# Two layers on one core: first loads in memory of their own, GpSimd's powers a step earlier, the scale inside the masked maximum

## What is computed

```
# part one: normalise x, shift, three projections r, k, v, scans along time -> rwkv
normed = (rwkv - mean) * rsqrt(var + 1e-5) * gamma + beta     # mean, var over all time steps of a head
x = x + normed @ W_o.T
# part two, on layernorm(x), twice
q, k, v = split(shift(h) @ wqkv)
q, k = l2norm(q) * qs, l2norm(k) * ks ; q, k = rotary_xpos(q, k)
sim = 8 * q @ k.T ; masked outside the window ; attn = softmax(sim) ; o = attn @ v
x = x + o @ wo
h = layernorm(shift(x)) * lg + lb ; x = x + (a * gelu(g)) @ w2 + b2,  a, g = split(h @ w1 + b1)
```

## Time and profile before

| | us |
|---|---|
| time, median of 3 runs (2927.34 to 2930.24) | 2929.16 |
| time of the profiled execution | 2932.18 |
| its span, first to last instruction | 2929.9 |
| PE busy (share of the span) | 2801.9 (96%) |
| ACT busy | 2325.5 (79%) |
| DVE busy | 2202.0 (75%) |
| POOL busy | 1571.2 (54%) |
| mean granted TensorE clock | 0.984 |

### The profile page before, as it was taken

The page is one execution under the profiler, slowest core; times in us unless marked ns, Lnnn a source line. Parts: engine busy times, 40 slices in busy tenths (PEclk is TensorE's granted clock), DMA queues, the critical chain, the costliest instruction groups (busy, mean ns, idle before and its releaser), DMA issues.

```text
span 2929.9 us, 67398 instructions
## 1 busy us (share of the span) xinstructions
PE 2801.9 (96%) x23076; PEld 2536.0 (87%) x23076; DVE 2202.0 (75%) x6587; ACT 2325.5 (79%) x5429; POOL 1571.2 (54%) x1524
## 2 busy tenths in 40 slices
PE   7999938899999999999999999999999999999998
PEld 6878826788998998899999899999999999999988
DVE  3979966887777778777777677777777777777773
ACT  4989946788888888888888788888888888888884
POOL 2313215656656665665566555555655655566553
PEclk9999968999999999999999999999999999999999
DMA  3252111111111111111111213111111111111111
GB/s 98 63 181 77 39 58 42 56 55 45 55 51 48 52 55 55 50 50 52 53 47 52 80 57 100 48 49 48 48 48 46 49 47 43 49 45 46 49 44 36
DMA packets 211302, 166.22 MB, mean 57 GB/s; under 512 B 21522, under 2 KB 206612, under 8 KB 209940
## 3 DMA queue, kind: packets, MB, share of 16 engines
q1 hardware_dynamic: 139284, 127.82, 14.3%
q10 hardware_dynamic: 71680, 34.10, 4.0%
HBM read 110.89 MB, written 42.58 MB: 52 GB/s over the span
## 4 chain that ended last, share of the span: by engine, by line
PE 64%; DVE 17%; POOL 6%; issue 6%; ACT 4%; DMA 1%; SPq 1%; DVEq 0%; ACTq 0%; POOLq 0%
PE ps L387 33%; PE ps L361 10%; PE ps L471 6%; PE ps L457 6%; DVE Sm L1072 5%; PE ps L445 5%; POOL rs L1218 3%; PE ps L430 2%; DVE Ar L1045 2%; POOL uTl L1304 1%; POOL r L1218 1%; DVE Gl L1145 1%; DVE Br L1046 1%; DVE Br L1047 1%; DVE oTl L1096 1%
## 5 line engine op out<-in xcount | busy, mean ns | idle before, releaser
L730 ACT ACTIVATE Sm<-Sm,nb,sc 128x256 f32<-128x256 f32 (+1 forms) x1024 | 597.4, 586 | 1.3 <-DVE nb L1079 0.5
L1072 DVE CUSTOM_DVE_ANT_0 Sm<-ps,mask 128x256 f32<-128x256 f32 (+1 forms) x1024 | 368.1, 414 | 79.6 <-PE ps L445 77.6
L387 PE MATMUL ps<-zTh,W1h 128*128 128x256 f32 (+1 forms) x1408 | 405.6, 288 | 0.0
L1145 DVE SCALAR_TENSOR_TENSOR Gl<-ps,vecs,Gl 128x256 f32<-128x256 f32 (+1 forms) x384 | 172.0, 475 | 304.2 <-PE ps L387 162.8
L387 PE MATMUL ps<-zTl,W1h 128*128 128x256 f32 (+1 forms) x1408 | 397.9, 283 | 0.0
L387 PE MATMUL ps<-zTh,W1l 128*128 128x256 f32 (+1 forms) x1408 | 393.4, 279 | 0.0
L1218 POOL TENSOR_TENSOR rs<-rs,mhalf 128x16 f32<-128x16 f32 x128 | 372.3, 2909 | 0.0
L710 ACT ACTIVATE sq<-ps 128x512 f32<-128x512 f32 x256 | 151.7, 593 | 261.7 <-PE ps L387 258.2
L1304 POOL TENSOR_TENSOR uTl<-Gl,uTh 128x512 fp32r<-128x512 f32 (+1 forms) x192 | 211.2, 1106 | 251.4 <-ACT uTh L798 199.1
L387 PE MATMUL ps<-WQh,hTh 128*128 128x512 f32 x768 | 341.5, 445 | 3.1 <-DVE hTl L1029 3.1
L387 PE MATMUL ps<-WQl,hTh 128*128 128x512 f32 x768 | 305.8, 398 | 0.0
(11 more groups left out here) (187 smaller groups left out, 8796.3 us busy)
## 6 DMA issues: line engine op xcount, KB each, us to landing
oF<-ro_scratch ACTq DMA_DIRECT2D x256, 128.0 KB, 3.0
tb<-tab SPq DMA_DIRECT2D x128, 128.0 KB, 2.3
xc<-x SPq DMA_DIRECT2D x32, 256.0 KB, 3.0
rwkv_scratch<-rw SPq DMA_DIRECT2D x32, 256.0 KB, 2.5
rk<-rwkv_scratch SPq DMA_DIRECT2D x64, 128.0 KB, 2.3
xin<-x SPq DMA_DIRECT2D x64, 128.0 KB, 2.2
x_scratch<-x SPq DMA_DIRECT2D x64, 128.0 KB, 1.7
y_scratch<-os SPq DMA_DIRECT2D x64, 128.0 KB, 4.0
```

What stands on the lines that cost most here:

```text
L387: ins = pe.matmul(dst, L(a), R(b), start=start and i == 0, stop=stop and i == 2)
L730: act.activation(Sm[:, h, c0:c1_], Sm[:, h, c0:c1_], ACT.Exp, bias=nb[:, h:h + 1], scale=sc[:, n % 4, h:h + 1], accum_out=sm[:, n % 2, h:h ...
L1072: dve.tensor_tensor_reduce(Sm[:, h, c0:c1_], PS[:, bank["scores", n, q, h % 2], (h // 2 % 2) * 256 + c0:(h // 2 % 2) * 256 + c1_], mask[:, ...
L1145: dve.scalar_tensor_tensor(out=Gl[0:v, j % 4, :], in0=s, scalar=V("b1a", 6 * l + j, 0, v), in1=gl, op0=ALU.add, op1=ALU.mult).then_inc(S[" ...
```

## The change

There are three groups of edits.

The tiles `mask`, `qsks`, `xin`, `rk`, `nF`, `nT`, `tb` and `rt` are allocated ahead of part one's tiles, so they share memory with nothing. SP issues the loads of mask, `qsks`, the first `rk` and the first `xin` in part one's last step, ahead of the last `store_rw`, and no longer waits for `end`. ACT waits for `g2` at 10 in place of `end` at 3. PE, DVE and POOL still wait for `end`.

On POOL `scale` moves from step n+3 to step n+2, right behind `rot`. Its power is cut in two, 8 values for k first, then the product of k, then 8 values for q; `sc` gets the factor -8. The steps behind it in the same turn of the loop are `table`, `zT_lo` (every other step) and `root0`.

On DVE the fused instruction takes `sc` as a scale per row, `Sm` = (scores + mask) x `sc`, with the minimum in place of the maximum, and leaves the result in `nb` itself; L1079 and `mx` are gone. ACT's `exp` has the constant scale -1. `pre_y` moves from the start of DVE's step to the place right behind the maxima.

```diff
+        mask = sb("mask", [2, 256])
+        qsks = sb("qsks", [2, 256])
...
         with ExitStack() as c1:
...
-            w.wait_ge(S["end"], 3)
+            w.wait_ge(S["g2"], 10)
...
-                w.wait_ge(S["nb"], 2 * n + q + 1)
+                w.wait_ge(S["mx"], 8 * n + 4 * q + 4)
...
-                                   scale=sc[:, n % 4, h:h + 1], accum_out=sm[:, n % 2, h:h + 1]).then_inc(S["ex"], 1)
+                                   scale=-1.0, accum_out=sm[:, n % 2, h:h + 1]).then_inc(S["ex"], 1)
...
-                        mask[:, n % 2, c0:c1_], 1.0, -3.0e38, ALU.add, ALU.max, mx[:, h:h + 1]).then_inc(S["mx"], 1)
...
-                dve.scalar_tensor_tensor(out=nb[:, r], in0=mx[:, r], scalar=-1.0, in1=sc[:, n % 4, r], op0=ALU.mult,
-                                         op1=ALU.mult).then_inc(S["nb"], 1)
+                        mask[:, n % 2, c0:c1_], sc[:, n % 4, h:h + 1], 3.0e38, ALU.add, ALU.min,
+                        nb[:, h:h + 1]).then_inc(S["mx"], 1)
...
-                if live(1) and t - 1 < NG:
-                    pre_y(t - 1)
...
                     masked_max(t - 4, 0)
                     masked_max(t - 4, 1)
+                if live(1) and t - 1 < NG:
+                    pre_y(t - 1)
...
-                inv_sqrt(rs[:, n % 2, :]).then_inc(S["rs"], 1)
+                inv_sqrt(rs[:, n % 2, 8:16]).then_inc(S["rs"], 1)
...
+                inv_sqrt(rs[:, n % 2, 0:8]).then_inc(S["rs"], 1)
+                w.wait_ge(S["rs"], 2 * n + 2)
...
-                if live(3):
-                    scale(t - 3)
...
                     rot(t - 2)
+                    scale(t - 2)
...
+                if t - 4 == NCH - 1:
+                    sp.dma_start(mask[:, :, :], mask_d).then_inc(S["ld2"], 16)
+                    sp.dma_start(qsks[:, :, :], qsk).then_inc(S["ld2"], 16)
+                    load_rk(0)
+                    load_x(0)
                 if 0 <= t - 4 < NCH:
                     store_rw(t - 4)
-
-            w.wait_ge(S["end"], 3)
```

More of the change, by code:

```diff
@@ L198, in build @@
         gsh = sb("gsh", [NB, 2])
+        mask = sb("mask", [2, 256])
+        qsks = sb("qsks", [2, 256])
+        xin = sb("xin", [2, 256])
+        rk = sb("rk", [2, 2, 128])
+        nF = sb("nF", [2, 128])
+        nT = pair("nT", [2, 128])
+        tb = sb("tb", [2, 256])
+        rt = sb("rt", [2, 256])
         def V(name, i, lo=0, hi=128):
@@ L1068, in masked_max @@
                 w.wait_ge(S["ld2"], 32)
+                w.wait_ge(S["sc"], n + 1)
+                w.wait_ge(S["ex"], 8 * (n - 1) + 4 * q + 4)
                 for h in (4 * q, 4 * q + 2, 4 * q + 1, 4 * q + 3):
```

44 lines of the change are left out of this document (14 added, 30 removed).

## The result

| | before | after |
|---|---|---|
| median of the runs (4 each) | 2929.7 us | 2907.56 us (2905.66 to 2908.88) |
| ratio after / before, 95% interval | | 0.9924 [0.9909, 0.9940] |
| span of the profiled execution | 2929.9 us | 2905.6 us |
| mean granted clock | 0.984 | 0.986 |

The change makes the kernel 22.1 us faster by the medians, 24.3 us by the spans. The forecast was 28.4 us of gain, 2900.8 us, with a range of 2888 to 2918, and faster.

What follows compares the result with a forecast made beforehand. PE's own work bounds the second layer; gains lie in the seam, filling and first layer. 5.9 + 15 + 7 + 0.5 (the end) = 28.4 us off 2929.16 gives 2900.8 us, range 2888 to 2918.

Steps and rivals of the forecast that it cites:

- The seam: Between the parts: with `rk` loaded early, `nTl` starts at 413.40 in place of 419.27, a gain of 5.9 us.
- The powers: POOL: a power of 8 values costs 1656 ns; PE's 11.8 us of waits for the product of k should go.
- The filling: 420 to 600 us, while the pipeline fills: PE's waits for the product of k and `x2` shrink, gaining 15 us.
- The lower bound of 6 us: Filling: gain if DVE's step, near 14 of 16 us, bounds at once; the rival that DVE or POOL does had 0.14.
- The first layer: PE's waits for DVE's rotary product, 10.9 us in all, shrink by 7 us.
- I take 0: DVE's fused maximum: the scale per row adds between 0 and 57 ns each, taken as 0.
- 4.9 us for each 10 ns: Price of a slower fused instruction, eight times per step on DVE, over about 61 steps of filling and first layer.
- the signs that were named for being wrong: Fused instruction above 430 ns or further apart, `y` far above 0.41 us, or a new first-layer PE wait over 1 us each.
- The port race: First layer: `y` 0.3 us later loses the port to POOL's `uTl` in 26 MLP steps, +15 us, 2923; chance 0.09.
- The slower instruction as the case on the other side: DVE's fused instruction with a scale per row is slower, deciding from 70 ns, 2956 at twice 57 ns; chance 0.06.
- ACT's `exp`: Loses a value per row, from 590 to about 500 ns; counted as cover, no time gained.
- The second layer: PE is never idle there (busy 799.90 of 800 us), so nothing is gained.

Runs made afterwards that it cites:

- y_idle_onepow: The changed kernel with `y` from step 12 on ahead of DVE's `glu` and one power of 16 values in place of two of 8; 2895.19 us, ratio 0.9883.
- mixed_onepow: The changed kernel with `y` ahead of `glu` from step 12, one power of 16, scale in the maximum for windows 0 to 7 only; 2891.66 us, ratio 0.9871.
- onepow: The changed kernel with one power of 16 values in place of two of 8, at the new place; 2903.28 us, ratio 0.9906.
- y_idle: The changed kernel with `y` from step 12 on ahead of DVE's `glu` instead of behind the maxima; 2898.33 us, ratio 0.9889.
- imm_scale: The changed kernel with the fused instruction multiplying by the constant -1 in place of the row's value `sc`; 2896.26 us, ratio 0.9883.
- no_seam: The changed kernel without the early loads: SP and ACT wait for `end`, first loads behind all stores; 2911.78 us, ratio 0.9937.
- y_old: The changed kernel with `y` back at the start of DVE's step, the powers at their new place; 3120.1 us, ratio 1.0649.
- scale_old: The changed kernel with `scale`, still cut in two, back in the later step behind `root1`; 2913.16 us, ratio 0.9939.
- seam_only: The kernel before with only the early loads, their own memory and ACT's wait for `g2`; 2923.26 us, ratio 0.9976.
- unfused: The changed kernel with the plain maximum, the small `nb` instruction and `exp`'s scale per row back; 2903.82 us, ratio 0.9911.
- y_idle_unfused: The changed kernel with `y` from step 12 on ahead of `glu` and the maximum without the scale, small `nb` back; 2896.07 us, ratio 0.9881.
- best: The changed kernel with `y` from step 12 on ahead of `glu`, the maximum without the scale and one power of 16; 2895.7 us, ratio 0.9884.

## Why the prediction was nearly right

**The seam: right.** Forecast 5.9 us and `nTl` at 413.4; measured 413.53 and a lead of 5.86, by itself worth a ratio of 0.9976. The early issues cost nothing, and the last store's end never showed.

**The powers: right in size.** A power of 8 values was put at 1656 ns and took 1647. The wait for the product of k went. `z` was to lose up to 0.5 us a step, half counted, which is 1.25 us in five steps. Only the first of the two `z` instructions of a window meets the product; it takes 0.83 us and not 0.35, so it loses 0.48, and in the filling that cost 1.5 us, in windows 7 to 9. The forecast was close here.

**The filling: right, 15 us forecast, 16.3 measured, and by its terms too, with some luck.** Forecast were 6 us where PE waits for the first two products of k; measured are 6.3 up to window 2. Forecast were 8 in the later steps, which have 6.9 from window 5 to 10; 2.3 come between and 0.7 behind. For the clock 1 us was counted: the 180 us of the filling have 0.91 and 0.92 of granted clock, 32.4 and 28.8 us at the lower level, so 1.8 us at most. The luck is in the sum: two kernels with the same instructions there (`y_idle_onepow` and `mixed_onepow`) differ by 2.5 us by their clock, so a match to 1.3 us is closer than one execution can promise. No run parts the new place of `y` from the cut of the power. The lower bound of 6 us gave DVE near 14 of a step's 16 us; the row named for it, 131.80 of 180 us, is 11.7 of 16.

**The first layer: the step that failed.** The term was 7 us; 2.4 came. The step was "I take 0" for the value per row of the fused instruction, with 57 ns as the far end. It is 62 ns, so the far end was the truth. The nearest row, L1145, which has such a value and a PSUM input, had said 475 ns; the reason for setting it aside, that it is another operation, was weak. The price of it was also wrong, the other way: 4.9 us for each 10 ns, on all 61 steps, would have made 29 us. Measured is 11 us by the time and 10.0 by the growth, since PE's wait in the first layer is only 0.28 us a time, and a DVE that is earlier by more than that gains nothing. The term had a second fault. It took PE's mean wait of 0.44 us as the thing to be shortened, but that mean is of 21 waits near 0.3 and four of 1.0 to 1.5; the four went, and the 21 needed DVE to be 0.3 us earlier, which it wasn't. Two of the signs that were named for being wrong did come: the fused instruction above 430 ns, and `y` far above 0.41 us. PE's wait for the rotary product came to 6.9 us, where about 3 was to show the forecast right.

**The port race: a rival that happened, at a lower price.** It was put at 0.3 us of delay for `y` and +15 us. `y` did come late, lost 0.41 us, and PE still waited 25 times; but `u_tail` (0.42 us) and `oT_lo` (0.69 us) ran free behind it. So PE's wait became 0.28 us and not 1.0. The race is part of what the first layer lacks against the kernel with the constant (8.1 us), not a loss against the kernel before; how large a part isn't shown.

**The slower instruction as the case on the other side: its place was right and its decision point not reached**, 62 ns against 70, and even there it would not have made a loss, by the price measured.

**ACT's `exp`:** forecast as cover, not time. It fell from 590 to 497 ns, and ACT from 828.54 of 1000 us to 782.11 of 984. The Trainium skill, page "ScalarE: Activation LUTs", section "What ACT_TABLE_LOAD costs", puts a pointer operand at about 93 ns: the trace agrees, 590 - 497 = 93. No time followed from it.

**The second layer: "nothing" was nearly right.** It came to 0.1 us, the sum of two things that nearly cancel: a gain of 1.75 us at the layer change, which goes with the granted clock and isn't of this change, and a loss of 1.6 us by the small change of pace below.

**What stays open.** In the second layer most pairs of windows take 37.24 us in the kernels with `exp` at a constant scale (after, onepow, y_idle, y_idle_onepow, imm_scale, no_seam, y_old, scale_old), and 37.18 or 37.19, some 37.11, in those with a scale per row (before, seam_only, unfused, y_idle_unfused, best, mixed_onepow), by the starts of the sums as above. The means of windows 70 to 124 are 37.17 to 37.21 against 37.13 to 37.17, with 37.180 for the changed kernel and 37.132 for the kernel before: over 32 pairs that is 1.5 us. It isn't the cut power, for `y_idle_onepow` has one power and 37.24, nor the value per row on DVE, for `imm_scale` has none there and 37.24. All kernels with `exp` at a constant scale also lack the small `nb` instruction, so the two can't be told apart. PE is busy throughout in the changed kernel and nearly so (799.90 of 800 us) in the kernel before; of its groups by line and form in the second layer's stretch the one below, of the changed kernel, has 308 ns, where the kernel before has 305. What makes PE slower there is not known; no run here tests it.

```profile
L387 PE MATMUL ps<-WOh,oTh 128*128 128x256 f32 x172 | 53.0, 308 | 0.0
```

## What to carry to other kernels

When an instruction grows by some ten nanoseconds on an engine with slack, don't price it by its length times its count only; see by how much the engine that waits for it is late, what now starts just behind a POOL instruction on SBUF, and whether it can stand in an idle stretch instead. An edit that moves work ahead of something on POOL has to be taken together with the edit that moves the consumer back: the change without the move of `y` was 190 us worse than the kernel before, not a few, while the change without the move of the powers was still 16 us better. Fusing a small instruction into four large ones saves busy time only if it costs each of them less than a quarter of what it saves; here it was 60 ns against 219 / 4 = 55. And before a gain of a few microseconds is put down to an edit, compare the granted clock in the stretch where it appears: here it went with 2.5 us between two kernels that had the same instructions there.
